# Expert feed-forward phase: the first bias added by VectorE, the first product one step further ahead, and one low half on GpSimd

## The reference, cut to what matters

```python
h = jnp.einsum('td,edh->teh', xf, w1) + b1      # 256 -> 512
h = _ln(h, ln1_g, ln1_b)                        # over the 512
h = jax.nn.gelu(h, approximate=False)
y = jnp.einsum('teh,ehd->ted', h, w2) + b2      # 512 -> 256
out = jnp.einsum('ted,te->td', y, combine)
```

## Time and profile before

| | |
|---|---|
| median of 3 runs | 2517.2 us (2516.88 to 2525.94) |
| the profiled execution: its own time | 2508.03 us |
| the profiled execution: span | 2506.3 us |
| busy in the span: PE, DVE, ACT, POOL | 87%, 68%, 55%, 51% |
| expert phase: first and last start of an instruction on its tokens' transposes | 1731.8 and 2266.8 us |
| from 1750 to 2270 us, 520 us: PE, DVE, ACT, POOL busy | 519.24, 392.30, 379.14, 222.99 us |
| granted TensorE clock in that stretch | 1.00 of full speed (2.4 GHz) |
| tail, 1640 to 1650 us and 1670 to 1680 us: transfers | 410 GB/s and 0 GB/s |

### The profile page before, as it was taken

One profiled execution on the slowest core, in us unless ns is written; L12 is line 12 of the kernel. 1 busy time (PEld: TensorE's weight loads), 2 busy tenths in 40 slices (PEclk: granted clock), 3 DMA queues, 4 the chain that ended last, 5 costly groups with the idle time before them and its releaser, 6 DMA issues. The chain is left out here.

```text
span 2506.3 us, 43240 instructions
## 1 busy us (share of the span) xinstructions
PE 2171.6 (87%) x12404; PEld 1503.9 (60%) x12404; DVE 1694.3 (68%) x4866; ACT 1366.7 (55%) x3316; POOL 1284.3 (51%) x1470
## 2 busy tenths in 40 slices
PE   2698998998999899899899899733999999996886
PEld 2454665555565565565555555222888888885665
DVE  2476687687587687587577678164777777772676
ACT  0155655655556556555555556421777777773333
POOL 1455465665555655654655755424444444444662
PEclk7799999999899999898899999755999999998998
DMA  3556556456556546645556555140222222223563
GB/s 115 126 125 148 115 120 155 113 120 159 110 111 157 124 111 155 124 110 144 106 120 146 129 117 130 21 158 19 69 69 69 69 68 66 69 69 99 164 181 118
DMA packets 192818, 281.98 MB, mean 113 GB/s; under 512 B 55736, under 2 KB 113720, under 8 KB 192592
## 3 DMA queue, kind: packets, MB, share of 16 engines
q1 hardware_dynamic: 173520, 236.14, 39.7%
q0 software_dynamic: 16768, 34.69, 5.0%
q10 hardware_dynamic: 2304, 8.39, 0.9%
HBM read 97.33 MB, written 37.56 MB: 54 GB/s over the span
## 5 line engine op out<-in xcount | busy, mean ns | idle before, releaser
L515 ACT ACTIVATE probs<-scores_T 128x512 f32<-128x512 f32 (+3 forms) x1536 | 654.6, 492 | 249.3 <-PE scores_T L405 234.9
L748 POOL TENSOR_SCALAR_AFFINE_SELECT probs<-probs 128x256 f32<-128x256 f32 x512 | 205.9, 410 | 529.6 <-ACT probs L515 526.9
L463 PE MATMUL ring<-k_stack,q_stack_b 96*128 96x512 f32 (+3 forms) x1024 | 396.0, 429 | 22.7 <-DVE neg_part L660 8.6
L660 DVE TENSOR_REDUCE neg_part<-ring 128x1 f32<-128x512 f32 x512 | 333.3, 683 | 95.8 <-PE ring L463 92.7
L405 PE MATMUL scores_T<-q_stack_b,k_stack 98*128 98x512 f32 (+3 forms) x1024 | 324.0, 394 | 43.6 <-ACT probs L515 42.8
L422 PE MATMUL o_ps<-probs,v_ones 128*17 128x512 f32 (+3 forms) x3072 | 348.6, 528 | 1.9 <-POOL probs L748 1.8
L463 PEld LDWEIGHTS ring<-k_stack,q_stack_b 96*128 96x128 f32 x1024 | 192.0, 196 | 227.0 <-issue 74.5
L665 DVE CUSTOM_DVE_ANT_0 ring<-ring,mask 128x384 f32<-128x384 f32 (+3 forms) x512 | 243.5, 507 | 116.3 <-PE ring L463 114.1
L665 DVE CUSTOM_DVE_ANT_0 ring<-ring,mask,neg_part 128x384 f32<-128x384 f32 (+3 forms) x512 | 260.5, 554 | 67.2 <-PE ring L463 66.8
L1066 ACT ACTIVATE g<-ht_ps,ln_b,ln_g 128x128 f32<-128x128 f32 x544 | 217.5, 449 | 135.9 <-PE ht_ps L1016 135.9
L405 PEld LDWEIGHTS scores_T<-q_stack_b,k_stack 98*128 98x128 f32 x1024 | 190.1, 202 | 103.1 <-ACT probs L515 75.9
(11 more groups left out here) (192 smaller groups left out, 4664.8 us busy)
## 6 DMA issues: line engine op xcount, KB each, us to landing
u_rot<-u SPq DMA_DIRECT2D x128, 256.0 KB, 3.8
k_stack<-u_rot SPq DMA_DIRECT2D x128, 256.0 KB
y_rows<-z SPq DMA_DIRECT2D x136, 128.0 KB
lat_w<-lat_split SPq DMA_DIRECT2D x32, 512.0 KB
q_stack_a<-u_rot SPq DMA_DIRECT2D x64, 256.0 KB
q_stack_b<-u_rot SPq DMA_DIRECT2D x64, 256.0 KB
k_stack<-u SPq DMA_DIRECT2D x64, 256.0 KB
x_raw<-in_xT SPq DMA_DIRECT2D x16, 512.0 KB, 4.5
```

Of the source, the lines that this page charges most:

```text
L463: nc.tensor.matmul(out[:, 0:k1 - k0], q_stack[qb // 4][0:3 * L, row_buf(n, qb // 4), h, P * (qb % 4):P * (qb % 4) + P], k_stack[0:3 * L, n ...
L515: nc.scalar.activation(probs[:, s % 2, h, cols], sc[(t + j) % 3][:, HALF - w:HALF], ACT.Exp).then_inc(exp_done, 1)
L660: nc.vector.tensor_reduce(neg_part[:, n % 2, part_col], src[:], AX_X, ALU.max, negate=True).then_inc(max_taken, 1)
L748: nc.gpsimd.affine_select(both, both, [[0, 2], [1, P]], ALU.is_ge, zero, base=0, channel_multiplier=-1).then_inc(kept, 1)
```

## The change

It has four parts. The first bias is no longer a matmul: the bias `b1` is loaded once into SBUF, repeated on all 128 partitions (2 MB there), and VectorE adds it while it moves the product from PSUM to `h_norm` in SBUF; moments and norm then work on `h_norm` in place, which now has three buffers. The first product and all ahead of it (transposes, `x_hi`, `x_lo`, the gather) are done one tile further ahead. The order of VectorE's turn is new. The second half of `g_lo` is formed by GpSimd, with a semaphore of its own. The memory for `g` comes from `o_sb`, a buffer of attention that is no longer used.

```diff
@@ routing tail (attention_phase)
-        b_raw, b_hi, b_lo = sb("b_raw", [E, H + C]), sb("b_hi", [E, H + C], F32R), sb("b_lo", [E, H + C], F32R)
+        b_raw, b_hi, b_lo = sb("b_raw", [E, C]), sb("b_hi", [E, C], F32R), sb("b_lo", [E, C], F32R)
...
+                sp.dma_start(experts["b1"][:], dram["b1"].unsqueeze(0).to_broadcast([P, E, H])).then_inc(ln1_loaded, 16)
...
-                nc.vector.memset(experts["b"][:].bitcast(F32), 0.0).then_inc(b_zeroed, 1)
+                nc.vector.memset(experts["b2"][:].bitcast(F32), 0.0).then_inc(b_zeroed, 1)
@@ expert_phase, GpSimd
-            for k in range(-5, MAX_TILES):
-                if tile(k + 5):
-                    j = k + 5
+            for k in range(-6, MAX_TILES):
+                if tile(k + 6):
+                    j = k + 6
...
-                if tile(k + 1):
-                    j = k + 1
+                if tile(k + 2):
+                    j = k + 2
                     pool.wait_ge(ve_done, j + 1)
...
+                if tile(k):
+                    pool.wait_ge(g_hi_ready, 2 * k + 2)
+                    nc.gpsimd.tensor_tensor(g_lo[k % 2][:, pairs[1], :], g[k % 2][:, pairs[1], :],
+                                            g_hi[k % 2][:, pairs[1], :].bitcast(F32),
+                                            ALU.subtract).then_inc(g_lo2_ready, 1)
@@ expert_phase, TensorE
-                        pe.wait_ge(g_lo_ready, 2 * j + i + 1)
+                        pe.wait_ge((g_lo_ready, g_lo2_ready)[i], j + 1)
...
-                        pe.wait_ge(h_norm_ready, j - 1)
+                        pe.wait_ge(h_added, j - 1)
...
-                    nc.tensor.matmul(h_ps[j % 2][:], routes["ones2"][:], experts["b"][:, bass.ds(e, 1), 0:H],
-                                     start=False, stop=True).then_inc(h_full, 1)
+                    last.then_inc(h_full, 1)
@@ expert_phase, VectorE
+                if tile(k + 2):
+                    j = k + 2
+                    e = dve.value_load(routes["expert"][0:1, j:j + 1], min_val=0, max_val=E - 1)
+                    dve.wait_ge(h_full, j + 1)
+                    if j >= 3:
+                        dve.wait_ge(ht_full, j - 2)
+                    nc.vector.tensor_tensor(h_norm[j % 3][:], h_ps[j % 2][:], experts["b1"][:, bass.ds(e, 1), :],
+                                            ALU.add).then_inc(h_added, 1)
                 if tile(k + 1):
                     j = k + 1
...
+                    nc.vector.tensor_scalar(h_norm[j % 3][:], h_norm[j % 3][:], h_mv[j % 2][:, 0:1],
+                                            h_rstd[j % 2][:, 0:1], ALU.subtract, ALU.mult).then_inc(h_norm_ready, 1)
```

More of the change, by code:

```diff
@@ L950, in expert_phase @@
         h_rstd = [sb(f"h_rstd{a}", [P, 1]) for a in range(2)]
-        h_norm = [sb(f"h_norm{a}", [P, H]) for a in range(2)]
-        g = [sb(f"g{a}", [P, FC, P]) for a in range(2)]
+        h_norm = [sb(f"h_norm{a}", [P, H]) for a in range(3)]
+        g = [tail["o_sb"][:, H * a:H * a + H].rearrange("p (f t) -> p f t", f=FC) for a in range(2)]
         g_hi = [sb(f"g_hi{a}", [P, FC, P], F32R) for a in range(2)]
@@ L1008, in expert @@
                 return pe.value_load(routes["expert"][0:1, j:j + 1], min_val=0, max_val=E - 1)
-            for k in range(-3, MAX_TILES + 1):
+            for k in range(-4, MAX_TILES + 1):
                 if tile(k):
@@ L1030, in _ @@
                                                  stop=False)
-                    nc.tensor.matmul(y_ps[j % 2][:, 0:C], routes["ones2"][:], experts["b"][:, bass.ds(e, 1), H:H + C],
+                    nc.tensor.matmul(y_ps[j % 2][:, 0:C], routes["ones2"][:], experts["b2"][:, bass.ds(e, 1), :],
                                      start=False, stop=True).then_inc(y_full, 1)
-                if tile(k + 3):
-                    j = k + 3
+                if tile(k + 4):
+                    j = k + 4
                     pe.wait_ge(x_in_loaded[j % 4], 16 * (j // 4 + 1))
@@ L1041, in _ @@
                     last.then_inc(xt_full, 1)
-                if tile(k + 2):
-                    j = k + 2
+                if tile(k + 3):
+                    j = k + 3
                     e = expert(j)
@@ L1046, in _ @@
                     if j >= 2:
-                        pe.wait_ge(h_norm_ready, j - 1)
+                        pe.wait_ge(h_added, j - 1)
                     for kc in range(KC):
                         for a, w in ((x_hi, "w1_hi"), (x_hi, "w1_lo"), (x_lo, "w1_hi")):
-                            nc.tensor.matmul(h_ps[j % 2][:], a[j % 2][:, kc, :], experts[w][:, bass.ds(e, 1), H * kc:H * kc + H],
-                                             start=kc == 0 and a is x_hi and w == "w1_hi", stop=False)
-                    nc.tensor.matmul(h_ps[j % 2][:], routes["ones2"][:], experts["b"][:, bass.ds(e, 1), 0:H],
-                                     start=False, stop=True).then_inc(h_full, 1)
+                            last = nc.tensor.matmul(h_ps[j % 2][:], a[j % 2][:, kc, :],
+                                                    experts[w][:, bass.ds(e, 1), H * kc:H * kc + H],
+                                                    start=kc == 0 and a is x_hi and w == "w1_hi",
+                                                    stop=kc == KC - 1 and a is x_lo)
+                    last.then_inc(h_full, 1)
         @block.scalar
         def _(act):
-            for k in range(-3, MAX_TILES + 1):
+            for k in range(-4, MAX_TILES + 1):
                 if tile(k):
@@ L1061, in _ @@
                     if k >= 2:
[L1062 removed]
+                        act.wait_ge(g_lo_ready, k - 1)
+                        act.wait_ge(g_lo2_ready, k - 1)
                         act.wait_ge(y_full, k - 1)
@@ L1088, in _ @@
             nc.vector.memset(routes["minus_half"][:], -0.5).then_inc(half_set, 1)
[L1090 to L1098, removed]
+            for k in range(-4, MAX_TILES):
+                if tile(k + 3):
+                    j = k + 3
                     dve.wait_ge(xe_hi_ready, j + 1)
@@ L1111, in _ @@
                 if tile(k):
[L1112 to L1120, removed]
-                    split_g(k, 1)
+                    dve.wait_ge(g_hi_ready, 2 * k + 1)
+                    nc.vector.tensor_tensor(g_lo[k % 2][:, pairs[0], :], g[k % 2][:, pairs[0], :],
+                                            g_hi[k % 2][:, pairs[0], :].bitcast(F32),
+                                            ALU.subtract).then_inc(g_lo_ready, 1)
 def combine_phase(nc, dram, routes, x1_dram, y_rows, out):
```

26 lines of the change are left out of this document (15 added, 11 removed).

## The result

The changed kernel took 2503.97 us (median of 8 runs, 2487.74 to 2511.76), the kernel before, run beside it, 2521.73 us (median of 8, 2516.88 to 2536.02). The ratio is 0.992, 95% interval 0.9893 to 0.9948: faster by 20 us of 2522, between 13 and 27. The prediction had 31, with a range of 14 to 37 (2503 and 2480 against the 2517.2 that it started from).

A forecast was written before the change was run, and what follows sets the result against it. TensorE was taken to bound the expert phase; -32.6 + 1.5 - 0.8 = -31.9 us on the profiled 2508.0 gave 2476, with the median 9 above it 2485.3, stated as 2486, range 2480 to 2503.

The forecast's parts named there:

- The mechanism that had 0.68: Expert phase: TensorE's own work stays the bound, at a turn of 3.65 to 3.75 us; chance 0.68.
- rival 1: GpSimd chain delays TensorE's second product in part of the turns: P about 3.80, gain 19 us, 2498; chance 0.17.
- What bounds the kernel now: Expert phase: TensorE, busy 519.24 of 520 us and not in the waits, sets the pace at 3.94 us a turn.
- the step of 0.33: TensorE, token transposes to first product: 0.33 instead of 0.13 in about half the turns, where the expert's number is read.
- The bias matmul goes: TensorE's first product: 136 bias matmuls of 0.24 removed, 32.6 us off, turn 3.94 to 3.70.
- The chain through GpSimd: From x_lo through VectorE and GpSimd to TensorE's second product: 8.22 us, allowing P = 3.56, slack 0.28 per two turns.
- 0.05 to TensorE: Last term of the 8.22 us chain: from GpSimd's subtraction end to TensorE's second product, 0.05 us.
- the three prices: VectorE's register read, addition and norm, which no row shows: taken at 0.6, 0.70, 0.55; upper ends 0.85, 0.81, 0.66.
- One step further ahead: Ends of the expert phase, first product one tile earlier: 0.5 lost at the start, 1.0 at the end, +1.5 us.
- The tail: Before the routing work: bias split and cast on a third of the columns, -0.8 us; 2 MB load 5 us, hidden.
- Rival 2: TensorE keeps its turn, the bias matmul having covered register reading: P = 3.90, gain 5 us, 2512; chance 0.08.
- Rival 3: VectorE held every turn by GpSimd's subtraction: its turn 4.11, 23 us slower, 2540; chance 0.07.

The follow-up runs named there:

- Run 5: The kernel before, with both register reads of TensorE's turn moved ahead of its first wait; expert phase 528.4 us, 20.6 shorter, timed ratio 0.994.
- run 1: The kernel before with only the first bias matmul taken out (bias left out of the result); expert phase 533.0 us, 16.0 shorter.
- run 4: The changed kernel with a matmul of the bias's size put back at the first product's end; expert phase 540.0 us, 12.4 longer.
- run 2: The changed kernel with GpSimd's subtraction placed ahead of the power; expert phase 513.8 us, 13.8 shorter; ratio to the kernel before 0.987.
- run 3: The changed kernel with both TensorE register reads ahead of its first wait; expert phase 513.8 us, 13.8 shorter; ratio to the kernel before 0.989.
- run 7: The changed kernel with the second g_lo back on VectorE behind the first; expert phase 504.9 us, 22.7 shorter; ratio to the kernel before 0.985.
- run 9: The changed kernel with both g_lo on VectorE and TensorE's register reads ahead of its first wait; expert phase 499.8 us.
- run 10: The changed kernel with both g_lo on VectorE, TensorE's reads first and VectorE's read ahead of its x_hi wait; 2476.99 us, ratio to the kernel before 0.980.
- run 8: The changed kernel without VectorE's register read, adding expert 0's bias for all tiles; expert phase 509.5 us, 18.1 shorter.

## Why the prediction was right, and where its sizes were off

The kernel is faster, as forecast, and the gain of 20 lies within the range of 14 to 37. (The median itself, 2503.97, is 1 us above the stated 2503; the kernel before stood 4.5 us higher beside it than when the range was drawn.) The mechanism that had 0.68, TensorE's own work as the bound at 3.65 to 3.75, is not what came: the turn is 3.81 (from 1850 to 2200 us). That the gain lies in the range is due to the range having been drawn out to rival 1, and so in part luck.

**What bounds the kernel now: wrong.** "TensorE is thus the engine that sets the pace" was read from a busy time of 519.24 in 520 us, and the step of 0.33 in half of the turns was seen and taken as given. "TensorE isn't in them" misreads the waits: the row `PEld h_ps L1050 <- issue` is there, 12.7 us in 59 times. It was the sign of a ring of two turns. Run 5 shows what TensorE's own work gives: 3.82.

**The bias matmul goes, 32.6 us: mis-sized.** It is 32.6 us of TensorE, but in the ring it counts once in two turns: 16.0 (run 1), and put back in the changed kernel 12.4 (run 4). The direction of the forecast was right since the change also altered the ring, to one of three turns, 11.47 us.

**The chain through GpSimd: right in its steps, wrong in its last term.** The chain was in the prediction, with a slack of 0.28 for two turns. By the trace the subtraction ends 8.33 after the transposes, where the prediction had 8.17. With 8.33 its own sum still gives P = (8.33 + 0.05 - 1.10) / 2 = 3.64, below 3.70, so the prices are not what failed. The term of "0.05 to TensorE" is the step that failed: TensorE's queue must have the subtraction early enough to issue what stands behind it, and from the subtraction's end to the first product are 1.65 us, of which seven matmuls and two transposes cover less than one (7 times 0.12 and 0.13). The rest, about 0.7, stands in the place of the 0.05, and the ring is 8.33 + 1.65 + 1.49 = 11.47 for three turns. The register read on VectorE was taken at 0.6 and was 0.82, inside its ends. Rival 1, "the chain through GpSimd touches in part of the turns", with 2498 and a turn of 3.80, is what came, at 0.17, by that chain but not for its reason: of the three prices that were to be near their upper ends only the read was, and the lead of TensorE's queue wasn't in it. Its signal, second products waiting for g_lo, came once in 350 us (0.3), since the lateness shows as "issue" one piece later.

**Prices.** From the changed kernel's lines of VectorE and GpSimd:

```profile
L1118 DVE TENSOR_SCALAR h_norm<-h_norm,h_mv,h_rstd x136: 535/538/1023, 1759.6 to 2270.6; 128x512 f32<-128x512 f32 x136
```

```profile
L994 POOL TENSOR_TENSOR g_lo<-o_sb,g_hi x136: 714/729/743, 1764.8 to 2276.4; 128x256 fp32r<-128x256 f32 x136
```

```profile
L990 POOL TENSOR_TENSOR h_rstd<-h_ve,minus_half x136: 567/674/684, 1758.1 to 2269.9; 128x1 f32<-128x1 f32 x136
```

The norm 0.54 (0.55 taken), the subtraction 0.73 (0.74), the addition 0.69 (0.70). The power is 0.67 and not 0.56: it runs beside VectorE's g_lo in 91 of 92 turns from 1850 to 2200 us, and in the one where it doesn't it took 0.57.

**One step further ahead: not borne out at the start.** From the first token transposes to the first copy it was 16.7 us and is 16.5, where 0.5 was added. The 1.0 at the end wasn't measured by itself.

**The tail: right.** The bias's low half took 0.41 and its cast 0.28. From VectorE's first cast of the tail (1640.60, now 1660.34) to the first transposes (1731.8, now 1750.9) are 91.2 and 90.6: -0.6 of the forecast -0.8. The load of 2 MB landed after 9.3 us and not 5, hidden.

**Rival 2** named the place, the growing step of 0.33, but with the bias as its cover; run 2, whose step shrinks without a bias matmul, and run 5 refute that. **Rival 3**, slower by the subtraction's holding, didn't come: the norm's median is 0.003 over its minimum. What there is of holding is the gather's, 0.02 a turn on the mean.

## What to carry to other kernels

A busy share near 1 on an engine doesn't show that its work sets the pace: compare the shortest turn with the mean one, and when turns alternate, add up a ring of as many turns as the pattern has. A register read behind a wait cost time here only when the wait ended late, so put it ahead of the wait; in the kernel before that was worth nearly as much as the whole change. Look then whether it has moved behind another late wait, as in run 3. Before work is moved to an idle engine, ask whether its end is in the ring, not how long the engine is idle.

## What the runs showed of the hardware

- TensorE's queue needs a lead in this kernel. A semaphore that arrived 0.29 us ahead of the matmul that needs it (subtraction's end 2005.25, 2005.54) made no wait there, but was followed by a step of 0.52 instead of 0.13 at the register read.
- The addition and x_lo, each with one operand in PSUM, weren't held by GpSimd's subtraction: 0.69 and 0.42 us with and without it beside them, in the changed kernel. VectorE's g_lo, both operands in SBUF, was: 0.96 for 0.42 in run 2. This agrees with the Trainium skill (SBUF — State Buffer, SBUF: two separate sides), by which an operation of VectorE with two SBUF inputs is shut out for the whole of an instruction of GpSimd that reads SBUF and started first.
- The norm, with one tensor operand in SBUF, took 0.56 to 0.73 for 0.54 in 22 of 91 turns of the changed kernel, and each time ended 0.22 or 0.23 after the end of GpSimd's gather. In runs 7, 9 and 10, where the two hardly meet, none took over 0.54.
- A register read ahead of the addition on VectorE: 0.82 from the start of the 0.42 us instruction ahead to the addition, and 0.34 without the read (run 8) or with it moved ahead (run 10).
- The expert phase began 19 us later from one execution to the next behind an attention with the same code, with the granted clock 0.93 for 0.94 from 100 to 1600 us.
